# One multi-matmul operation split into single matmuls with their own waits, at the first group of three matmul stages

## The reference

```python
x_conv = silu(causal_conv4(x) + conv_b)
q, k, v = x @ Wq.T, x @ Wk.T, x @ Wv.T           # 16 heads of 128
gate = sigmoid(x_conv @ gate_w.T + gate_b)
q, k = l2norm(q), l2norm(k)
S_t = gamma * S_(t-1) + k_t * v_t                # elementwise scan over tokens
y = (gate * S * q) @ Wo.T                        # then a layer norm with ln_w, ln_b
# ffn
hidden = silu(x @ W1.T) * (x @ W3.T)             # 8192 wide
out = fwht(hidden) @ W2.T                        # Walsh-Hadamard transform, then W2
```

## Time and profile before

| | |
|---|---|
| Time, median of 3 runs | 3404.28 us (lowest 3404.23) |
| Profiled execution, its own time | 3403.7 us |
| Its span on the slowest core (core 4) | 3401.2 us |
| Spans of the eight cores | 3392.3 to 3401.2 us |
| Mean granted TensorE clock, core 4 | 0.899 of full |

### The profile page before, as it was taken

One profiled execution on the slowest core, in us unless ns is written; L12 is line 12 of the kernel. 1 busy time (PEld: TensorE's weight loads), 2 busy tenths in 40 slices (PEclk: granted clock), 3 DMA queues, 4 the chain that ended last, 5 costly groups with the idle time before them and its releaser, 6 DMA issues.

```text
span 3401.2 us, 33915 instructions; the slowest of 8 cores (3392.3 to 3401.2 us)
## 1 busy us (share of the span) xinstructions
PE 2439.6 (72%) x10322; PEld 1008.0 (30%) x10322; DVE 1069.2 (31%) x1669; ACT 523.8 (15%) x868; POOL 683.4 (20%) x839
## 2 busy tenths in 40 slices
PE   2227666678989877621688887829998788783899
PEld 0002222233333332200233333304433333331343
DVE  1865555511212110277212313180001213316300
ACT  0201111243333322211111111100001111110000
POOL 0330000022323220023222313141111313315111
PEclk9657888889999999855899999969999899997999
DMA  6012222224343432100667676628887677673798
GB/s 149 1 25 38 44 43 38 37 44 69 56 69 56 69 50 45 18 0 0 111 103 121 112 123 112 112 44 139 143 139 121 103 118 119 111 124 56 130 178 162
DMA packets 81134, 283.31 MB, mean 83 GB/s; under 512 B 9280, under 2 KB 13378, under 8 KB 80962
## 3 DMA queue, kind: packets, MB, share of 16 engines
q0 software_dynamic: 75584, 264.28, 47.3%
q1 hardware_dynamic: 5378, 16.88, 1.5%
HBM read 536.97 MB, written 8.39 MB: 160 GB/s over the span
## 4 chain that ended last, share of the span: by engine, by line
PE 60%; DVE 17%; issue 11%; ACT 5%; POOL 3%; DMA 2%; DVEq 1%; SPq 1%; another core or an unknown queue 0%; ACTq 0%; POOLq 0%
PE pb L853 13%; PE pb L784 13%; PE pb L790 12%; PE pb L538 8%; PE pb L651 3%; PE pb L441 3%; DVE f L803 2%; PE pb L449 2%; DVE f L377 2%; PE pb L807 1%; DVE lnxb L764 1%; DVEq L111 1%; DMA wpool<-w 1%; PE pb L353 1%; DVE x_sb L702 1%
## 5 line engine op out<-in xcount | busy, mean ns | idle before, releaser
L784 PE MATMUL pb<-xcv,wpool 128*128 128x512 bf16 x2048 | 479.1, 388 | 50.8 <-DVE xcv L379 26.9
L790 PE MATMUL pb<-xcv,wpool 128*128 128x512 bf16 x2048 | 462.9, 379 | 0.0
L280 POOL DMA_DIRECT2D wpool<-w x384 | 203.8, 532 | 1287.6 <-PE pb L784 513.5
L853 PE MATMUL pb<-slotA,wpool 128*128 128x512 bf16 x1024 | 308.8, 383 | 138.6 <-DVE f L750 66.8
L803 DVE TENSOR_TENSOR f<-sq,pb 128x512 bf16<-128x512 bf16 x128 | 87.9, 687 | 857.1 <-PE pb L790 856.4
L538 PE MATMUL pb<-lnxb,wpool 128*128 128x512 bf16 x1536 | 347.3, 385 | 0.0
L853 PE MATMUL pb<-lnxb,wpool 128*128 128x512 bf16 x1024 | 308.3, 383 | 0.0
L784 PEld LDWEIGHTS pb<-xcv,wpool 128*128 128x128 bf16 x2048 | 195.6, 99 | 294.6 <-issue 76.9
L790 PEld LDWEIGHTS pb<-xcv,wpool 128*128 128x128 bf16 x2048 | 200.3, 98 | 241.7
L538 PEld LDWEIGHTS pb<-lnxb,wpool 128*128 128x128 bf16 x1536 | 149.5, 99 | 188.7 <-issue 19.6
L799 ACT ACTIVATE sq<-pb 128x512 bf16<-128x512 f32 x128 | 76.5, 597 | 715.4 <-PE pb L784 709.9
(11 more groups left out here) (163 smaller groups left out, 2367.7 us busy)
## 6 DMA issues: line engine op xcount, KB each, us to landing
wpool<-w POOLq DMA_DIRECT2D x384, 512.0 KB, 5.9
wpool<-wk POOLq DMA_DIRECT2D x32, 512.0 KB, 6.2
wpool<-wv POOLq DMA_DIRECT2D x32, 512.0 KB, 6.2
x_sb<-x SPq DMA_DIRECT2D x1, 8192.0 KB
wpool<-wq POOLq DMA_DIRECT2D x16, 512.0 KB, 9.4
wpool<-wg POOLq DMA_DIRECT2D x16, 512.0 KB, 7.3
wpool<-wo POOLq DMA_DIRECT2D x16, 512.0 KB, 5.1
out<-x_sb SPq DMA_DIRECT2D x16, 512.0 KB, 7.9
```

The source lines that it names most:

```text
L280: P.dma("gpsimd", lambda E, view=view, dram_ap=dram_ap: E.dma_start(out=view, in_=dram_ap), writes=[key], sem=f"GW{slot}")
L784: mm = E.matmul(pg[:, :], wv1[:, c * 128:(c + 1) * 128], lnx2_view(c, s), start=(c == 0), stop=(c == NCH - 1), skip_group_check=True)
L790: mm = E.matmul(pl[:, :], wv3[:, c * 128:(c + 1) * 128], lnx2_view(c, s), start=(c == 0), stop=(c == NCH - 1), skip_group_check=True)
L853: mm = E.matmul(po[:, :], wv[:, ci * 128:(ci + 1) * 128], hsb_view(c), start=(pos == 0), stop=(pos == FCH - 1), skip_group_check=True)
```

## The change

At h = 0 of the Wo stage and at f = 0 of both feed-forward passes, the function that issues 16 matmuls is replaced by 16 operations of the plan with one matmul each. Each reads only its own chunk's key, of its own half, and writes the bank's key. In the feed-forward pass the gate and the linear matmuls of one chunk are issued in turn (gate c, linear c), where before all 16 gate matmuls stood ahead of the 16 linear ones. The waits for attn_all and lnx2_all are gone. Other groups are as before.

```diff
-                    def mms(E, wv=wv, s=s, pbank=pbank):
-                        for c in range(NCH):
-                            mm = E.matmul(pbank[:, :], wv[:, c * 128:(c + 1) * 128], slotA_view(c, s),
-                                          start=(c == 0), stop=(c == NCH - 1), skip_group_check=True)
-                        return mm
-                    P.op("tensor", mms, reads=[kw] + (attn_all if h == 0 and s == 0 else []),
-                         writes=[kbank])
+                    if h == 0:
+                        for c_ in range(NCH):
+                            P.op("tensor", lambda E, wv=wv, c_=c_, s=s, pbank=pbank: E.matmul(
+                                pbank[:, :], wv[:, c_ * 128:(c_ + 1) * 128], slotA_view(c_, s),
+                                start=(c_ == 0), stop=(c_ == NCH - 1), skip_group_check=True),
+                                reads=[kw, ("attnb", c_, s)], writes=[kbank])
+                    else:
+                        ...
+                        P.op("tensor", mms, reads=[kw], writes=[kbank])
...
-                    P.op("tensor", mg, reads=[kw1] + (lnx2_all if (f == 0 and s == 0) else []), writes=[kpg])
-                    P.op("tensor", ml, reads=[kw3], writes=[kpl])
+                    if f == 0:
+                        for c_ in range(NCH):
+                            P.op("tensor", lambda E, wv1=wv1, c_=c_, pg=pg, s=s: E.matmul(
+                                pg[:, :], wv1[:, c_ * 128:(c_ + 1) * 128], lnx2_view(c_, s),
+                                start=(c_ == 0), stop=(c_ == NCH - 1), skip_group_check=True),
+                                reads=[kw1, ("lnx2", c_, s)], writes=[kpg])
+                            P.op("tensor", lambda E, wv3=wv3, c_=c_, pl=pl, s=s: E.matmul(
+                                pl[:, :], wv3[:, c_ * 128:(c_ + 1) * 128], lnx2_view(c_, s),
+                                start=(c_ == 0), stop=(c_ == NCH - 1), skip_group_check=True),
+                                reads=[kw3, ("lnx2", c_, s)], writes=[kpl])
+                    else:
+                        P.op("tensor", mg, reads=[kw1], writes=[kpg])
+                        P.op("tensor", ml, reads=[kw3], writes=[kpl])
```

More of the change, by code:

```diff
@@ L647, in build_nc, with mms @@
                     pbank, kbank = pb[bi], (f"pb{bi}",)
-                    def mms(E, wv=wv, s=s, pbank=pbank):
-                        for c in range(NCH):
-                            mm = E.matmul(pbank[:, :], wv[:, c * 128:(c + 1) * 128], slotA_view(c, s),
-                                          start=(c == 0), stop=(c == NCH - 1), skip_group_check=True)
-                        return mm
-                    P.op("tensor", mms, reads=[kw] + (attn_all if h == 0 and s == 0 else []),
-                         writes=[kbank])
+                    if h == 0:
[5 more added lines that the diff above has]
+                    else:
+                        def mms(E, wv=wv, s=s, pbank=pbank):
+                            for c in range(NCH):
+                                mm = E.matmul(pbank[:, :], wv[:, c * 128:(c + 1) * 128], slotA_view(c, s),
+                                              start=(c == 0), stop=(c == NCH - 1), skip_group_check=True)
+                            return mm
+                        P.op("tensor", mms, reads=[kw], writes=[kbank])
                     extra = P.retire("lnx", "lnxH") if first_yb[0] else []
```

## The result

The changed kernel takes 3431.0 us in the median, the one before 3404.3 us (executions in which one half of the chip ran slower are left out of all medians and ratios here, and e1's trace is read on the half that ran as usual): the ratio is 1.0079, 95% interval 1.0067 to 1.0091, so it is 23 to 31 us slower, 27 by the ratio. Forecast were 3420 us and a range from 3411 to 3431. The measured time lies at the upper end of that range, by the ratio 0.2 us beyond it (3431.2), and the interval reaches well to both sides of that end. The direction is right, the size is not: 16 us forecast, 27 measured. The profiled execution took 3427.2 us with a span of 3425.7 on core 3, 24.5 more than the span of before.

What follows compares the result with a forecast made beforehand. TensorE, with 60% of the chain that ended last, was taken as the bound. Wo h = 0 +9.0, feed-forward s = 0 +4.1 and s = 1 +3.0 make 16.1 us; on 3403.7 that gives 3420 us, range 3411 to 3431.

Steps and rivals of the forecast that it cites:

- Nothing gained at Wo's start: Wo, h = 0: L651 still starts at 1248.13, because the wo load is the last to come.
- A matmul behind an own wait costs 0.54 us a step at 2.4 GHz: Single matmuls writing one bank: each waits on TensorE's own semaphore for the one before, 0.54 us apart, not 0.216.
- The clock in Wo h = 0: Wo, h = 0: clock rises to 2.4 GHz after 4.6 us again; +4.15 and +4.85, together +9.0 us.
- low-clock rival: Wo, h = 0: clock stays at 1.2 GHz through both groups, h = 1 pays the rise; total +24.8, 3428.5 us; chance 0.28.
- The interleaved pairs: Feed-forward f = 0, gate and linear in turn: 0.30 us a matmul, bounds 0.27 and 0.32; at s = 1 +3.0 us.
- the upper bound: Layer norm's sums, alternating between two banks at 0.32 us a matmul, taken as upper bound for interleaved feed-forward matmuls.
- Feed-forward, s = 0: f = 0: linear 0 waits for w3[0]'s landing, silu and table load uncovered, L803 later by 4.1 us.
- The range: Whole kernel: 3411 to 3431 us, from half-priced own waits up to the low clock with its margin.
- Own waits free: Wait on itself costs nothing; only order and uncovered silu remain: 2.4 + 0.5 = +2.9, 3406.6 us; chance 0.14.

Runs made afterwards that it cites:

- e1: Only the change's Wo-stage edit, against the kernel before: ratio 1.0049 (1.0025 to 1.0073), 16.7 us slower.
- e7: Kernel before, with loads of wo[0] to wo[2] moved ahead of the last head's elementwise work, w1[0] and w3[0] ahead of the layer norms: ratio 0.9974, median 3399.1 us.
- e4: Kernel before with the change's Wo edit at h = 0 and also at h = 8, feed-forward unchanged: single time 3437.4 us.
- e3: Changed kernel without TensorE's wait on its own semaphore behind the first matmul of a group: ratio 1.0020 (0.9995 to 1.0045), median 3407.9 us.
- e6: Kernel before, only f = 0 changed: single gate matmuls without own waits, then the whole linear group; one run at 3401.3 us, no usable comparison.
- e8: Changed kernel, own waits and interleaving included, with earlier loads of wo[0] to wo[2], w1[0] and w3[0]: ratio 0.9992 to before, median 3402.0 us.
- e5: Kernel before with the Wo edit alone, two matmuls in each operation: one time, 3422.1 us, with no run of before to compare.
- e9: Kernel before with earlier wo, w1 and w3 loads, single-matmul operations without own waits, and gate before linear: ratio 0.9941, median 3386.8 us.
- e11: e9 with ScalarE's square of the first Wo group written to f0 instead of sq0: ratio 0.9929 to before, median 3383.0 us.

## Why the prediction was wrong

*Nothing gained at Wo's start*: right. L651 is released by the wo landing in both, and e7 shows it from the other side.

*A matmul behind an own wait costs 0.54 us a step at 2.4 GHz*: right, 0.525 to 0.54 in e4, though no core had 2.4 GHz in the changed kernel's Wo groups. At 1.2 GHz it was sized at 0.79 and is 0.73: I took the 0.632 us of a matmul in a stream, and a lone one lasts 0.58.

*The clock in Wo h = 0*: this is the step that failed. The sum assumed that the clock would rise 4.6 us into the group "again", as under a stream, and had +9.0 us for it. It stayed at 1.2 GHz on all eight cores for both groups, and h = 1 paid for the rise: +16.2 us. The low-clock rival has just this mechanism, with 17.7 us where 16.2 were measured; it had 0.28 and the forecast 0.50. No row of before decided between them, as the prediction said; the choice of the cheaper one was mine and was wrong. e3 shows that without the own waits the clock does rise in the first group, and e4 that even a chain that starts at 2.4 GHz loses it.

*The interleaved pairs*: mis-sized. Taken at 0.30 us a matmul, they take 0.34 to 0.35: at s = 1 the 32 matmuls and the silu take 11.6 us, where 10.3 was forecast; +4.3 for +3.0. The 0.27 that 0.54 / 2 gives was not reached, and no run shows why; the sums of the layer norm, at 0.32, were not the upper bound that I made of them.

*Feed-forward, s = 0*: w3[0]'s landing as the new bound, the uncovered table load and silu: all there. Forecast +4.1, measured +2.9 to the first product on the mean of the cores (+5.0 on core 3, 14.35 for 9.30 there before). The landing was read on one core in one execution: linear 0 was to start 1.2 us behind the layer norm's end, and does so on core 3 (1.1), but on the seven others it starts 0.3 to 1.9 us ahead of it, w3[0] having landed sooner. The clock rises 3.4 us behind linear 0 on core 3 and 4.4 to 5.6 us behind it on the others. And +1.6 that the prediction did not have: TensorE idles 2.84 us for the silu and the product, and f = 1 runs in part at 1.2 GHz; at s = 1 the same costs 0.4 more. The work that an exposed wait uncovers isn't its only price.

*The range*: its upper end was the low-clock case (3428.5) and 2.5 us. The distances add up to +25.4 us, for +24.8 in that case, so it has the size as well as the mechanism, but partly by luck: it has Wo 1.5 us and the start of s = 0 1.2 us too dear, the pairs at s = 1 1.3 us too cheap, and the clock at f = 1 (1.6 and 0.4) not at all. Where the last 1.5 us between 25.4 and the ratio's 26.9 lie, no run shows; the interval is 8 us wide.

*Own waits free*: refuted by e3. Without them the kernel is 2 us (distances) or 3 us (medians) slower than before, as that rival has it for the change (+2.9); with them it is 27.

## What to carry to other kernels

Before a stage's inputs are waited for piece by piece, see what releases its first instruction: here it was a weight load queued behind the data's producer, and moving the load (e7) gave 7 us where the finer waits gave none. When a group of accumulating matmuls is cut into operations, look at what the dependency tracker adds between them: here a write after a write of the same engine, whose order the traces show without the wait too, cost 0.3 us a matmul and the clock on top. And two groups that are interleaved both end at the end, so the work that ran beside the second has to find other cover: gate before linear, with the same fine waits, brought −4.5 us in the traces (e6).

## What the runs showed of the hardware

- A chain of lone 128×512 matmuls, each issued 0.15 us after the last one's end, left TensorE at 1.2 GHz for 25 us on all eight cores (after). Begun at 2.4 GHz, it lost that clock on all eight cores: after 10.5 to 11.3 us on seven in e4 (1.1 on one), after 8.7 us on seven in e8 (18.9 on one).
- With an own wait behind every second matmul, cores of one execution went both ways: 22 us on two of them, 29 to 30 on five (e5).
- A lone matmul at 1.2 GHz lasts 0.58 us in the rows, one in a stream 0.63.
- Behind interleaved pairs with own waits and a pause of 2.84 us, the next group started at 1.2 GHz on all eight cores (4.8 to 5.3 us for 3.61, after); behind a dense stream and a pause of 2.96 us, on four of eight (e3).
- Increments and already met waits on every matmul cost 0.024 us each in one group (e3, 3.99 for 3.63 us over 16) and nothing in others (e3 at s = 1, 0.216 us apart; the first Wo group of e9 and e11, 3.62 us).
